# Reversing the stage order of a software pipeline, and making two one-time waits unconditional, in a pre-layernorm attention and FFN kernel

## What is computed

```python
# layer 0, per batch element x [2048, 1024], 16 heads of 64
h    = layernorm(x)                       # no scale, no shift
Q, K, V = h @ Wq + bq, h @ Wk + bk, h @ Wv + bv
s    = Q K^T / 8 + mask                   # mask: -0.25 * log(i - j), -inf above the diagonal
x    = x + softmax(s) V @ Wo + bo
h2   = layernorm(x)
real, imag = split(h2)
x    = x + concat(real @ WR^T - imag @ WI^T + bR, real @ WI^T + imag @ WR^T + bI)
```

## Time and profile before

| what | value |
|---|---|
| time, median of 2 runs | 1252.18 us (1250.02 to 1254.35) |
| the profiled execution's own time | 1246.62 us |
| its span, core 4, the slowest | 1245.0 us (cores 1226.7 to 1245.0) |
| PE busy | 775.1 us (62%) |
| DVE busy | 583.3 us (47%) |
| ACT busy | 421.4 us (34%) |
| POOL busy | 176.4 us (14%) |
| mean granted TensorE clock, core 4 | 0.802 |

### The profile page before, as it was taken

How to read it: one execution, slowest core, us unless ns; L and a number is a source line. 1 busy time by engine, 2 the same in 40 slices (tenths; PEclk the granted TensorE clock), 3 DMA queues, 4 the chain that set the end, 5 groups by cost and what they waited for, 6 DMA issues and landing times.

```text
span 1245.0 us, 13322 instructions; the slowest of 8 cores (1226.7 to 1245.0 us)
## 1 busy us (share of the span) xinstructions
PE 775.1 (62%) x3636; PEld 262.4 (21%) x3672; DVE 583.3 (47%) x1179; ACT 421.4 (34%) x667; POOL 176.4 (14%) x136
## 2 busy tenths in 40 slices
PE   0011179696786776866768768766375757575656
PEld 0000024331131221312212213111021212122212
DVE  4555433247447465474563554644326333434332
ACT  0011010054665656657556667666300000000000
POOL 2212300014113040130241000000002001101000
PEclk9999988896686978968866889776866777777767
DMA  4111330424122021130220000000411020200101
GB/s 109 51 53 59 62 47 1 51 81 89 35 34 69 1 52 51 11 92 1 52 68 1 1 1 2 1 1 1 92 28 50 1 102 34 84 29 23 67 35 68
DMA packets 39391, 52.50 MB, mean 42 GB/s; under 512 B 21782, under 2 KB 23830, under 8 KB 39192
## 3 DMA queue, kind: packets, MB, share of 16 engines
q1 hardware_dynamic: 16856, 36.95, 9.2%
q0 software_dynamic: 22464, 14.68, 7.2%
HBM read 51.63 MB, written 8.39 MB: 48 GB/s over the span
## 4 chain that ended last, share of the span: by engine, by line
PE 45%; DVE 15%; ACT 10%; issue 10%; DMA 8%; another core or an unknown queue 5%; DVEq 3%; POOL 3%; ACTq 0%; SPq 0%; POOLq 0%
PE qk L377 8%; PE psF L955 7%; ACT PTb L636 6%; DMA xrot<-x 6%; PE pv L693 6%; PE stP L610 6%; PE psW L888 4%; PE pr L708 4%; DVE PTb L669 4%; DVE stat L220 3%; POOL sqscr L218 2%; DVEq L409 2%; PE qk L485 2%; DVE xnrot L256 2%
## 5 line engine op out<-in xcount | busy, mean ns | idle before, releaser
L636 ACT ACTIVATE PTb<-stP,negCS 128x1024 bf16<-128x1024 f32 x224 | 244.4, 1110 | 226.0 <-PE stP L616 223.9
L663 DVE TENSOR_TENSOR PTb<-PTb,decayS 128x512 bf16<-128x512 bf16 (+1 forms) x320 | 142.7, 446 | 251.0 <-ACT PTb L636 196.3
L693 PE MATMUL pv<-PTb,V 128*64 128x512 bf16 (+1 forms) x320 | 139.9, 437 | 102.9 <-DVE PTb L669 97.4
L610 PE MATMUL stP<-QTs,KTs 64*128 64x512 bf16 (+1 forms) x320 | 137.0, 434 | 24.6 <-ACT PTb L636 22.7
L242 ACT ACTIVATE stat<-stat 128x1 f32<-128x1 f32 x32 | 6.5, 203 | 424.1 <-DVEq L237 424.1
L669 DVE TENSOR_TENSOR PTb<-PTb,decayS 128x512 bf16<-128x512 bf16 (+1 forms) x320 | 144.9, 453 | 3.8 <-issue 0.2
L701 PE MATMUL pv<-PTb,V 128*64 128x512 bf16 (+1 forms) x320 | 144.3, 451 | 0.0
L714 PE MATMUL pr<-PTb,ones 128*64 128x512 bf16 (+1 forms) x320 | 139.8, 438 | 0.0
L708 PE MATMUL pr<-PTb,ones 128*64 128x512 bf16 (+1 forms) x320 | 139.5, 437 | 0.0
L616 PE MATMUL stP<-QTs,KTs 64*128 64x512 bf16 (+1 forms) x320 | 137.6, 435 | 0.0
L300 PE MATMUL psT<-identS,xnrot 128*128 128x128 bf16 x128 | 16.2, 307 | 143.2 <-DVEq L260 143.2
(11 more groups left out here) (95 smaller groups left out, 1016.8 us busy)
## 6 DMA issues: line engine op xcount, KB each, us to landing
xrot<-x SPq DMA_DIRECT2D x28, 512.0 KB, 3.8
g1b<-g1rep SPq DMA_DIRECT2D x32, 256.0 KB, 2.7
g2b<-g2rep SPq DMA_DIRECT2D x32, 256.0 KB, 3.0
out<-outbuf SPq DMA_DIRECT2D x4, 1024.0 KB, 4.9
out<-outbuf POOLq DMA_DIRECT2D x4, 1024.0 KB, 4.5
xrot<-x POOLq DMA_DIRECT2D x4, 512.0 KB, 4.0
Wqp<-wq POOLq DMA_DIRECT2D x8, 256.0 KB, 4.8
Wkp<-wk POOLq DMA_DIRECT2D x8, 256.0 KB, 5.8
```

The costliest lines, as they stand in the source:

```text
L610: P.emit("tensor", lambda t, j=j, pi=pi, mt=mt, c=c, no=no: t.matmul(stP[j][:, no:512], KTs[0:64, pi * SEQ + mt * 128:pi * SEQ + (mt + 1) ...
L636: s.activation(PTb[:, slot * 1024:(slot + 1) * 1024], stP[j][:, 0:1024], AF.Exp, bias=negCS[:, pi:pi + 1]),
L663: P.emit("vector", lambda v, slot=slot, off=off, no=no: v.tensor_mul(PTb[:, slot * 1024 + no:slot * 1024 + 512], PTb[:, slot * 1024 + no:s ...
L693: t.matmul(pv[0:64, no:512], V[:, mt * 1024 + h0 * 64:mt * 1024 + h0 * 64 + 64], PTb[:, slot * 1024 + no:slot * 1024 + 512], start=(mt == ...
```

## The change

Two edits. First, the waits that held only for the first step or group are now given each time: `emit_mult` always waits for `ae_decay` behind its exponential, and `emit_attnV` with mt = 0 always waits for `v_done` and `ve_ones`. Second, the five parts of an iteration of the output stage are called in reverse: C(i-4), B(i-3), B_ln(i-2), B_stats(i-1), A(i). Which tile a part works on in an iteration stays the same.

```diff
@@ emit_mult
                         decayS[:, off + no:off + 512]),
-                        waits=([(aE, erh[k]), (aE, ae_decay)]
-                               if (p == 0 and k == 0) else [(aE, erh[k])]))
+                        waits=[(aE, erh[k]), (aE, ae_decay)])
@@ emit_attnV
                     if mt == 0:
-                        if p == 0 and c == 0:
-                            wv_.append((vE, v_done))
-                            wv_.append((vE, ve_ones))
+                        wv_.append((vE, v_done))
+                        wv_.append((vE, ve_ones))
                         if pvpr_free is not None:
                             wv_.append(pvpr_free)
@@ output stage
             for i in range(NT + 4):
+                if 4 <= i and i - 4 < NT:
+                    stageC(i - 4)
+                if 3 <= i and i - 3 < NT:
+                    stageB(i - 3)
+                if 2 <= i and i - 2 < NT:
+                    stageB_ln(i - 2)
+                if 1 <= i and i - 1 < NT:
+                    stageB_stats(i - 1)
                 if i < NT:
                     stageA(i)
-                if 1 <= i and i - 1 < NT:
-                    stageB_stats(i - 1)
-                if 2 <= i and i - 2 < NT:
-                    stageB_ln(i - 2)
-                if 3 <= i and i - 3 < NT:
-                    stageB(i - 3)
-                if 4 <= i and i - 4 < NT:
-                    stageC(i - 4)
```

## The result

The changed kernel takes 1188.41 us (median of 11 runs, 1184.49 to 1193.3); the kernel before, run beside it, 1248.76 us (median of 10). The ratio is 0.952, with a 95% interval from 0.950 to 0.955. The profiled execution took 1188.41 us, its slowest core is core 6 with a span of 1186.9 us (cores 1165.9 to 1186.9).

What follows compares the result with a forecast made beforehand. The output stage was taken as bound by a chain, with PE waiting while DVE's order put statistics before normalisation. Full iterations +58, fill +21, drain -5.5 gain 74 us; waits cost 10: 1188 us median, range 1158 to 1214.

Steps and rivals of the forecast that it cites:

- The sum: Whole kernel: output stage gains 74 us, added waits cost 10, together -64 us.
- The gap: Output stage: PE idles 2.41 us, or 2.84 with the drain instruction, between FFN product and transposes; mean 2.62.
- The price of the clock: Output stage: slow matmuls after each gap lose 2.4 us on average, making the period 15.1 instead of 12.7 us.
- Fill and drain: Output pipeline's ends: fill 35 us instead of 56.3, gaining 21; drain 38.0 instead of 32.5, losing 5.5.
- The load of x: Output stage, four iterations: residual add late by 0.8 us behind SP's output DMA, nothing waits; the old stall goes.
- The waits: Attention stage: added waits on DVE's first multiply and PE's first attention products cost 10 us together.
- 105 x 0.08 = 8.4 us: Attention stage: one more wait costs 0.08 us at each of 105 multiplies on the critical path.
- the attention stage some 10 us longer: Sign that would show the forecast right: added waits lengthen the attention stage by some 10 us.
- The rule on idle gaps: Output stage: skill's rule that short PE gaps keep the upper clock; as rival, 1148 us, chance 0.12.
- The rule on semaphores: Attention stage: by the skill's rule added waits cost nothing, time 10 us lower; prediction rejected it for a waiting engine.
- The rival of the held normalisation: Output stage: POOL's square delays the normalisation up to 1.9 us per period, 23 us, giving 1211 us; chance 0.10.

Runs made afterwards that it cites:

- e2: The kernel before with only the output stage's parts reversed, without the added waits: 1185.1 us, ratio 0.948 to the kernel before.
- e6: Reversal without the added waits, plus twelve discarded matmuls between each FFN product and the transposes: 1139.26 us, ratio 0.913 to the kernel before.
- e8: The kernel before with all eight output DMAs issued by POOL instead of every second one by SP: 1232.32 us, ratio 0.986.
- e4: The kernel before with eight satisfied waits ahead of the first attention product of each group, on PE: 1256.22 us, ratio 1.005.
- e1: The changed kernel with the output stage's parts in their old order, so the added waits alone: 1252.72 us, ratio 1.003 to the kernel before.
- e7: The kernel before with two stages moved, so the statistics come behind the normalisation; Wo product still ahead of the transposes: 1169.11 us, ratio 0.937.
- e5: Reversal without the added waits, with the normalisation put ahead of the output add in DVE's list: 1113.26 us, ratio 0.890 to the kernel before.
- e3: The kernel before with five satisfied waits added ahead of every first multiply instead of one: 1299.51 us, ratio 1.040.
- e10: Reversal without the added waits, with drain and output DMA moved behind the copy of the transposes: 1169.51 us, ratio 0.937 to the kernel before.

## Why the prediction was right, point by point

- *The sum.* -64 us against -60 by the ratio (0.952 of 1249). Both terms were too large, and since their signs are opposite the errors partly cancel: that the total is only 4 us off is in part luck. The reversal gives 0.948 in e2, 65 us (62 by the medians) of the 74 forecast, and the waits cost 4 to 5 us of the 10. In the traces of the slowest cores the output stage gives 67.5 of the 74: 55 of 58 in the full iterations, 22 of 21 in the fill, and the drain loses 10 where 5.5 were forecast.
- *The gap.* 2.41 and 2.84 us were forecast from the drain, and these are the gaps after the change. The drain of the old pipeline had the new order in it already.
- *The price of the clock.* 2.4 us for each gap was forecast, and 15.1 us for a period. Core 6 shows 184.3 / 12 = 15.4. The mean was nearly right; that it is 1.1 us behind the short gap (13.6 - 12.5) and 4.2 behind the long one (17.1 - 12.9), where the two cases of the earlier trace rows gave 1.6 and 3.2, was not foreseen, so the mean is in part luck too. That the slow matmuls come from the gap was argued from two cases; e6 shows it.
- *Fill and drain.* 35 us forecast for the fill, 34.2 measured. 38.0 for the drain, 42.4 on core 6, where the last step took 13.3 us; six of the eight cores show 39.1.
- *The load of x.* The late residual add waits 0.75 us and holds nothing up, as forecast (0.8). The prediction counts four iterations with a late load; every core has three, since no load is left behind the fourth output DMA of SP. e8 shows that SP's order was the cause before, worth 1.4% on its own. The reversal takes the same three gaps away, so this is part of its 65 us, and not on top of them.
- *The waits.* The step that was oversized is "105 x 0.08 = 8.4 us". The price of a wait is 0.07 us (0.08 came from rows rounded to 0.01). The count came from L669, the second multiply, but L669 is on the chain also where it waits for a second exponential of its own (L649, on the diagonal), and there the wait of L663 is hidden. The chain of waits from 260 to 890 us has some 90 pieces of L669 but 82 of L663; 82 x 0.07 = 5.7 us. With e4's 1.4 that is 7, above the 4 to 5 measured, but inside e1's interval (0.4 to 8 us). The sign "the attention stage some 10 us longer" came out at half: from the first multiply to the first Wo matmul it is 652.5 us before, 656.7 in e1 and 657.7 after the change (medians over the eight cores).
- *The rule on idle gaps.* By the Trainium skill, TensorE: Matmul & The Clock Gate (Why this matters for your kernels), such short gaps keep the upper clock, and the time would have been 1148 us. The trace disagrees: gaps of 2.84, 2.41 and in e7 even 1.87 us are followed by matmuls at 1.2 GHz (3.45 us for eight at 1067.01), though not every one is (e7's drain, above). Its advice, to keep PE busy continuously, is what e5 and e6 bear out.
- *The rule on semaphores.* By the Trainium skill, VectorE: DVE Perf Modes (The DRAIN you can't avoid) semaphores in a back-to-back row are free. For a wait on an engine that stands idle e3 shows 0.07 us each.
- *The rival of the held normalisation.* L256 takes 0.80 to 0.82 us everywhere after the change, so nothing came of it there. But the mechanism exists, and the one that starts second is the one that takes longer. In e10 the square starts first and L256 takes up to 1.60 us (1090.61 and 1091.45 above), six times. In e5 L256 starts first and takes its 0.81 us, and the square takes 2.27 us instead of 1.89; so it is in all 120 such pairs in the traces of nine kernels, eight of them after the change, one on each core. In its other periods the square is over before C ends, as the prediction argued.

```profile
1041.66 0.81 DVE L256 TENSOR_SCALAR xnrot<-x,stat 128x1024 bf16<-128x1024 f32 x1
1041.95 2.27 POOL L218 TENSOR_TENSOR sqscr<-x 128x1024 f32<-128x1024 f32 x1 [5.78 <-DVE x L903]
```

## What to carry to other kernels

In a software pipeline on in-order engines, look at which operations stand between two uses of the bounding engine, and put there only what that use needs; the others go beside its work. Here moving the statistics gave 65 to 80 us (e2, e7), and one more operation (e5) another 72, since it closed the gap altogether. Where a short idle time is followed by matmuls at the lower clock, count it about twice on average, as here; single gaps of 2.4 to 2.9 us cost from nothing to 4.4 us more than their length. A wait that is needed once should be given once: on a waiting engine each costs 0.07 us, and in a loop on the critical path this is measurable.

## What the runs showed that I had not expected

- Twelve useless matmuls in each gap make the kernel 46 us faster (e6 against e2), because they keep PE at 2.4 GHz.
- Four more waits ahead of the multiply cost 46 us, and one costs 4: the mean clock of the attention stage is 0.71 with them and 0.78 without.
- POOL's square holds up L234, a 128x1 tensor by tensor operation (1.37 us, against 0.16). It holds L256, a tensor by scalar operation of 1024 columns, only where the square started first (up to 1.60 us in e10); where L256 started first it takes 0.81 us and the square grows from 1.89 to 2.27 us (e5). The sum L213 beside it keeps its 1.21 us.
- With PE busy 98% of the time or more on all eight cores, the granted clock is 1.00 over the 120 us of e5's full iterations.
